# Non-local attention block on one core: reads of the shared PSUM bank moved two steps behind TensorE, a tenth ring slot, four chunks of g ahead of the first image

## The reference

```python
x = x + block(group_norm(x, 32 groups))        # x: 4 images, 256 channels, 4096 positions
# block, for one image, xn = the normalised image as a 256 x 4096 matrix:
g    = g_w @ xn + g_b                          # 128 x 4096
f    = xn.T @ xn                               # 4096 x 4096, symmetric
attn = softmax(f, axis=-1)
y    = attn @ g.T                              # 4096 x 128
wy   = W_w @ y.T + W_b                         # 256 x 4096
wy   = (wy - mean) * rsqrt(var + 1e-5) * gamma + beta   # mean, var over all images and positions
return wy + xn
```

## Time and profile before

| | us |
|---|---|
| median of 3 runs | 2197.24 (2196.96 to 2199.29) |
| profiled execution | 2195.28 |
| its span, first to last instruction | 2193.5 |
| PE busy | 2059.5 (94%) |
| DVE busy | 1556.7 (71%) |
| ACT busy | 1090.8 (50%) |
| POOL busy | 810.7 (37%) |
| chain that ended last | PE 68%, issue 11%, POOL 8%, ACT 5%, DVE 4%, DMA 3% |
| products of f (L1135, L1136, L1137) on PE | 512.8 + 433.1 + 436.1 |
| takes (L930, L938) on DVE | 395.7 + 269.0 |

### The profile page before, as it was taken

The page is one execution under the profiler, slowest core; times in us unless marked ns, Lnnn a source line. Parts: engine busy times, 40 slices in busy tenths (PEclk is TensorE's granted clock), DMA queues, the critical chain, the costliest instruction groups (busy, mean ns, idle before and its releaser), DMA issues.

```text
span 2193.5 us, 32307 instructions
## 1 busy us (share of the span) xinstructions
PE 2059.5 (94%) x9348; PEld 1454.6 (66%) x9348; DVE 1556.7 (71%) x3123; ACT 1090.8 (50%) x2234; POOL 810.7 (37%) x623
## 2 busy tenths in 40 slices
PE   5899999989999999999999999998999999999988
PEld 4686777755577777765667677765558777766433
DVE  5576777777766777786767677777776677777656
ACT  3344455555444445447444445545544444555644
POOL 3001223459602023448631122445850102345840
PEclk9999999999999999999999999999999999999999
DMA  3112234545512323554522223464541233346969
GB/s 139 77 77 81 103 121 130 173 150 178 178 45 87 115 98 110 165 175 138 197 72 93 87 92 112 129 200 137 191 150 49 87 120 102 110 130 218 344 236 356
DMA packets 108408, 304.50 MB, mean 139 GB/s; under 512 B 11584, under 2 KB 11968, under 8 KB 93888
## 3 DMA queue, kind: packets, MB, share of 16 engines
q1 hardware_dynamic: 108224, 302.30, 40.6%
HBM read 159.65 MB, written 142.61 MB: 138 GB/s over the span
## 4 chain that ended last, share of the span: by engine, by line
PE 68%; issue 11%; POOL 8%; ACT 5%; DVE 4%; DMA 3%; DVEq 0%; SPq 0%; POOLq 0%; ACTq 0%
PE bank L1201 12%; PE bank L1135 10%; PE bank L1137 9%; PE bank L1136 9%; PE bank L1177 7%; PE bank L1205 4%; PE bank L1207 4%; PE bank L1206 4%; POOL fy_d L695 3%; POOL fy_c L695 3%; ACT ring L760 2%; PE bank L1350 2%; PE bank L1271 2%; DVE plo L965 2%; DMA fy_c<-spill 2%
## 5 line engine op out<-in xcount | busy, mean ns | idle before, releaser
L786 ACT CAST phi<-bank 128x512 fp32r<-128x512 f32 x480 | 281.9, 588 | 765.7 <-PE bank L1177 764.7
L930 DVE TENSOR_SCALAR_CACHE_REDUCE ring<-bank 128x512 f32<-128x512 f32 x576 | 395.7, 688 | 209.3 <-PE bank L1137 164.0
L1135 PE MATMUL bank<-xh 128*128 128x512 f32 (+3 forms) x1152 | 512.8, 445 | 8.4 <-POOL xl L668 6.4
L1137 PE MATMUL bank<-xh,xl 128*128 128x512 f32 (+3 forms) x1152 | 436.1, 379 | 0.0
L965 DVE TENSOR_TENSOR plo<-bank,phi 128x512 fp32r<-128x512 f32 x480 | 327.2, 685 | 153.5 <-ACT phi L786 121.2
L1136 PE MATMUL bank<-xl,xh 128*128 128x512 f32 (+3 forms) x1152 | 433.1, 376 | 0.0
L1177 PEld LDWEIGHTS bank<-ident,ring 128*128 128x128 f32 x1920 | 231.6, 142 | 183.4 <-issue 109.2
L760 ACT ACTIVATE ring<-ring,nmax 128x512 f32<-128x512 f32 x480 | 345.8, 722 | 0.0
L1177 PE MATMUL bank<-ident,ring 128*128 128x128 f32 x1920 | 295.1, 277 | 43.7 <-DVE plo L965 22.5
L695 POOL TENSOR_TENSOR fy_d<-fy_d,maxrow 128x512 f32<-128x512 f32 x188 | 242.3, 1291 | 222.3 <-DMA fy_d<-spill 222.3
L695 POOL TENSOR_TENSOR fy_c<-fy_c,maxrow 128x512 f32<-128x512 f32 x200 | 259.0, 1297 | 167.0 <-DMA fy_c<-spill 166.6
(11 more groups left out here) (115 smaller groups left out, 2716.9 us busy)
## 6 DMA issues: line engine op xcount, KB each, us to landing
spill<-ring SPq DMA_DIRECT2D x112, 1024.0 KB, 4.4
fy_c<-spill SPq DMA_DIRECT2D x200, 256.0 KB, 4.1
fy_d<-spill SPq DMA_DIRECT2D x188, 256.0 KB, 4.1
ring<-x_dram SPq DMA_DIRECT2D x40, 512.0 KB, 4.9
lbuf<-spill SPq DMA_DIRECT2D x60, 256.0 KB, 4.0
yd<-yn SPq DMA_DIRECT2D x32, 256.0 KB, 3.4
fx_a<-x_dram SPq DMA_DIRECT2D x16, 512.0 KB, 8.3
out_dram<-fx_a SPq DMA_DIRECT2D x16, 512.0 KB, 4.6
```

The lines of the kernel that those rows point to most:

```text
L786: nc.scalar.copy(phi[:, HI_BUF[n], :], whole(p)).then_inc(hi_made, 1)
L930: last = nc.vector.tensor_scalar(ring[:, SLOT[u], t, :], src, 1.0, None, ALU.mult, ALU.max, accum_out=rowm[:, t, c:c + 1])
L1135: nc.tensor.matmul(dst, xh[:, k, rows], xh[:, k, cols], start=(k == 0), stop=False)
L1137: last = nc.tensor.matmul(dst, xl[:, k, rows], xh[:, k, cols], start=False, stop=(k == K - 1))
```

## The change

- `add_g`, `count_wy` and, for rows 1 to 5, `merge_max` move from one step to two steps after PE's part (`merge_max` after the last take: from 0 or 1 to 2). `count_wy` and `invert` move ahead of the takes, `invert` also ahead of the additions of left tiles.
- g: both halves of a chunk are made in one step, the second in the bank `lacc` instead of `sps`. In the head of image 0 four chunks (`FIRST_G`) instead of two are made before the first step, and the exponentials (from step -7) stand ahead of `gh` on ACT.
- A tenth slot, which lies in the first two rows each of `fy_c` and `fy_d`. Only chunk (1, 4) uses it. Products of row 1 are spread over 22 steps instead of 25: the last is made in step 21 (before: 25), of row 2 in step 50 (before: 53).
- The first exponentials of the next image start in step 249 instead of 251, one in each step.
- Normalising starts one step later (`GROUP_AT`), and the cast (`make_xh`) follows the normalisation (`make_xn`) by a step.

```diff
-SLOTS = 9
+SLOTS = 10
+ROW_SLOT = 9
@@ SLOT
-        8, 0, 4, 1, 5, 6, 7,
-        2, 3, 8, 0, 4, 1,
-        5, 6, 7, 2, 3,
+        8, 0, 4, 9, 1, 5, 6,
+        7, 2, 3, 8, 0, 4,
+        5, 6, 7, 1, 2,
@@ plan_products
-        steps = range(PRODUCTS_FROM[j], PRODUCTS_FROM[j] + {1: 25, 2: 19, 3: 18, 4: 18, 5: 18, 6: 2 * n, 7: 2 * n}[j])
+        steps = range(PRODUCTS_FROM[j], PRODUCTS_FROM[j] + {1: 22, 2: 19, 3: 18, 4: 18, 5: 18, 6: 2 * n, 7: 2 * n}[j])
-            step = where[q * len(where) // n]
+            step = where[q * len(where) // n] if j > 1 else steps[q * len(steps) // n]
+            if c == j and t > 1:
+                step = max(step, made[-1] + 1)
+            if SLOT[u] == ROW_SLOT:
+                step = max(step, 2 * T)
-MERGE_STEP = {j: COLS_STEP[j] + (1 if j > 1 else 0) for j in range(1, NB)}
+MERGE_STEP = {j: COLS_STEP[j] + (2 if j < 6 else 1) for j in range(1, NB)}
-FIRST_EXP = -5
+FIRST_EXP = -7
-GROUP_AT = STATS_STEP[-1] + 2
+GROUP_AT = STATS_STEP[-1] + 3
-G_AT = {T * (c - 1) - 2 + h: (c, h) for c in range(2, NB) for h in range(2)}
+G_AT = {T * (c - 1) - (1 if c < NB - 1 else 0): c for c in range(2, NB)}
-SPARE_FROM = {c: max(p for p in SPLIT if tile(p)[1] == c) + 1 for c in range(NB - 1)}
+SPARE_FROM = {c: last_use(LAST_IN_SLOT[ROW_SLOT]) + 1 if c < 2 else max(p for p in SPLIT if tile(p)[1] == c) + 1
+              for c in range(NB - 1)}
-LAST_HEAD_G = G_AT[max(s for s in G_AT if s < HEAD)]
+LAST_HEAD_G = G_AT[max(s for s in G_AT if s < HEAD)], 0
+FIRST_G = range(LAST_HEAD_G[0])
@@ send, on SP
+                if SLOT[u] == ROW_SLOT:
+                    for h, rows in enumerate((fy_c, fy_d)):
+                        sp.dma_start(spill[pair(*CHUNKS[u]), :, 2 * h:2 * h + 2, :],
+                                     rows[:, 0:2 * W].rearrange("p (t w) -> p t w", w=W)).then_inc(spilled[ROW_SLOT], 16)
@@ step, on ACT
-                if s - 1 in G_AT and G_AT[s - 1][1] == 1:
-                    make_gh(b, G_AT[s - 1][0], first)
+                if s - 2 in G_AT:
+                    make_gh(b, G_AT[s - 2], first)
-                    make_xh(b + 1, XN_OF[s])
+                    make_xn(b + 1, XN_OF[s])
+                if more and s - 1 in XN_OF:
+                    make_xh(b + 1, XN_OF[s - 1])
@@ head, on ACT
-            for c in NEXT_G:
-                make_gh(0, c, first=True)
             for s in range(FIRST_EXP, 0):
                 for x3 in EXPS_AT[s]:
                     exp_right(0, *x3)
+                if s + LAG == 0:
+                    for c in NEXT_G:
+                        make_gh(0, c, first=True)
@@ add_g, on DVE (make_g on PE likewise)
+                made = lacc if h == 1 and (first or c not in NEXT_G) else sps
@@ step, on DVE
                 if p in SPLIT_NO:
                     split_lo(b, p, first)
+                if j >= 1 and i == INVERT_AT + LATE[j - 1]:
+                    invert(b, j - 1)
+                if tail and i == INVERT_AT + 1:
+                    invert(b - 1, NB - 1)
                 for w in ADDS_AT[p]:
                     add_left(b, w)
-                if p - 1 in G_AT:
-                    add_g(b, *G_AT[p - 1])
+                if p - 2 in G_AT and not (first and G_AT[p - 2] in FIRST_G):
+                    for h in range(2):
+                        add_g(b, G_AT[p - 2], h)
                 if more and p - 1 in NEXT_G_AT:
                     add_g(b + 1, *NEXT_G_AT[p - 1])
-                if j >= 1 and i == INVERT_AT + LATE[j - 1]:
-                    invert(b, j - 1)
+                if j >= 1 and i - 2 in WY_AT:
+                    count_wy(b, j - 1, WY_AT.index(i - 2))
...
-                if j >= 1 and i - 1 in WY_AT:
-                    count_wy(b, j - 1, WY_AT.index(i - 1))
@@ head, on DVE (on PE likewise)
-            for c in NEXT_G:
+            for c in FIRST_G:
                 for h in range(2):
-                    add_g(0, c, h)
+                    add_g(0, c, h, first=True)
@@ make_g, on PE
+                elif h == 0 or c in NEXT_G:
                     shared_free(b, "g", c, h)
+                elif c > len(NEXT_G):
+                    pe.wait_ge(g_added, b * (2 * NB) + 2 * c)
+                else:
+                    pe.wait_ge(left_taken, b * (NB - 1))
```

66 lines of the change are left out of this document (38 added, 28 removed).

## The result

The changed kernel takes 2146.69 us (median of 4 runs, 2145.51 to 2148.12) against 2197.39 us (4 runs, 2196.96 to 2199.29) of the kernel before: ratio 0.9768, 95% interval 0.9751 to 0.9785. The change wins 50.7 us; 40.7 us were forecast. The time lies in the forecast's own range, 2140 to 2172 us. Not all terms of the sum lie in theirs: blocks 1 to 3 won far more than their upper bound, and block 5 lost time where a gain was forecast.

What follows compares the result with a forecast made beforehand. TensorE, busy 94% of 2193.5 us, bounds the kernel; about 90 us of its waits, apart from the clock, are the ceiling. Terms 12.0+2.8+9.5+3.0+7.8+3.0+5.0-2.4 = 40.7 us, from 2197.24 to 2156.5 us; own range 2140 to 2172, stated range 2140 to 2184.

Steps and rivals of the forecast that it cites:

- End of block 0: Steps 22 to 31, four images: 4.5 us of PE waits less 1.5 for ACT, 3.0 us an image, 12.0 in all.
- the pairs: Pairs of products in steps 8 to 11, two takes a step: cost 0.6 us an image, 2.4 us; bounds 0 and 8.
- Seam: Hardware loop's seam after step 11: a second half of g covers PE's low-half stop; 1.4 us at two seams, 2.8 us.
- Head: Head of image 0: eight halves of g in two banks, exponentials earlier, step 0 at 84.5 us; 9.5 us, bounds 6 and 12.
- The three parts: Head: step 0 earlier 5.0 us, four halves less in later steps 3.7, clock 1.8; together 10.5, less 1.0.
- Blocks 1 to 3: Merges two steps behind shorten PE's waits behind merges and exponentials: 0.75 us an image, 3.0 us; bounds -1 and 6.
- Block 5: Inverse ahead of additions 1.2 us, normalising and cast later 1.4; 2.6 us in three images, 7.8 us; bounds 0 and 14.
- Block 6 and the end of an image: Block 6: 1.0 us in three images, 3.0 us. Image ends: exponentials earlier 2.7, no half clock 2.3, sum 5.0 us.
- (a): DVE's queue bounds more often; only head and image ends gain, 14.5 us, elsewhere waits change name: 2183 us; chance 0.25.
- (b): Slower: PE waits for unread shared bank 7, ten times an image; 55 us loss against 40.7 gain: 2211 us; chance 0.06.
- (c): Block 0: the 22-step product plan does the work, the slot little; changes no time; no chance of its own given.
- One sign that I had named for being wrong: DVE waiting as long as before under another name; no size given.

Runs made afterwards that it cites:

- the two kernels with nine slots: Changed kernel without the tenth slot, with the old product plan: merges near 0.9901, 2175.6 us; merges two steps behind 0.9817, 2157.2 us.
- The square above: Slot against merge distance, near then two steps behind: nine slots 2175.6 and 2157.2 us; ten slots 2170.8 and 2146.4 us (the changed kernel).
- group statistics early: Changed kernel with group statistics and normalising one step earlier, where they were before, the cast still one step behind: 0.9733, 2138.7 us.
- the run with two chunks: Changed kernel with two chunks of g in the head of image 0 instead of four: 0.9771, 2147.1 us.
- merges near: Changed kernel, slot kept, merges where they were before (rows 2 to 5 one step behind the last take, row 1 in its step): 0.9879, 2170.8 us.
- the combined kernel: Changed kernel with group statistics one step earlier, row 6 and 7 merges two steps behind, g chunk 7 in step 22, inverse behind additions: 0.9684, 2128.0 us.
- the kernel with nine slots and far merges: Changed kernel with nine slots and the old product plan, merges still two steps behind the last take: 0.9817, 2157.2 us.
- the kernel with nine slots and near merges: Changed kernel with nine slots, the old product plan and merges where they were before: 0.9901, 2175.6 us.

## Why the prediction was right, and where not

**What bounds the kernel.** Right: the gain came out of PE's waits, for which 90 us were named as the ceiling. Of its clock it kept little: the 20.5 us at half clock in the head, in block 0 and at the end of image 2 are gone, and as many came back around step 176.

**End of block 0.** Forecast 3.0 us an image (4.5 less 1.5 for ACT), and 0.6 us off for the pairs. Blocks 0 of images 1 to 3 won 5.0 to 5.6 us. In steps 26 to 31 one stop of 1.76 us is left of 4.5 us, so that part is 2.8 us, the mechanism and nearly the size. I called ACT late next, with 1.5 us; it is ACT, though by way of GpSimd's low half of g. What I missed lies in front of step 25: steps 0 to 24 fell from 83.70 to 81.80 us, although the transposes of the column maxima moved in, where I had booked a cost of 0.6. The pairs of products cost nothing that shows. The gain in steps 0 to 24 comes neither from the slot nor from the merges: in image 3 steps 0 to 24 take 79.70 and 79.71 us in the two kernels with nine slots, 79.93 in the changed kernel and 82.02 before. Nor from the inverse (79.95 us with it behind again). What is left are g and the projections, to which I had given nothing outside the seam; 0.65 us of it are the projections'. No run takes g's part back by itself. The square above corrects the reason for the rest: I ascribed the gain to the earlier plan; the distance of the merge carries more of it.

**Seam.** Forecast 2.8 us, by an extra 0.92 us of PE to cover the low half. It failed. From step 11 to 13 the seams of images 1 and 2 cost 1.93 and 2.22 us more than the same steps of image 3 before, and 1.89 and 1.93 now: 0.3 us won. After step 11 PE stops 1.68 us (image 1) where it stopped 1.27. First the low half of the kernel before, then the changed kernel:

```profile
644.48 0.69 DVE L965 TENSOR_TENSOR plo<-bank,phi 128x512 fp32r<-128x512 f32 x1 [1.46 <-PE bank L1207]
...
629.60 0.68 DVE L993 TENSOR_TENSOR plo<-bank,phi 128x512 fp32r<-128x512 f32 x1
...
631.41 0.65 PE L1214 MATMUL bank<-ident,ring 128*128 128x128 f32 x4 [1.68 <-issue]
```

The low half ends at 630.28 us, PE starts 1.1 us later with nothing to wait for that the profile shows. In some of the kernels above the profile still names the low half, but there too it ends 0.6 to 1.0 us before PE starts (group statistics early: 625.21 and 626.17 us), while in step 176 of that kernel 0.06 us pass. Already in the kernel before it ended at 645.17 us and PE started at 645.78; the bracket names the releaser, not the distance. So the step that failed is taking this stop for a wait for the low half. It looks like PE's own way through the end of the loop, which covering the low half can't shorten; no run takes the loop away, so this is read from the rows, not tried.

**Head.** Forecast step 0 at 84.5 us; it is at 86.1. But head and block 0 of image 0 won 15.3 us. Less the 5.3 us that other images win in block 0, 10.0 are the head's, against 9.5; by the run with two chunks 2.8 of them hang on the two additional chunks. The three parts shift among themselves: 3.4 us up to step 0 in place of 5.0; the stop in front of it is the 1.05 us below (before: 4.26), and the clock stays at the upper level from 29.6 to 452.9 us, where before it was at half from 83.2 to 93.4 and again from 175.4 to 178.8 us.

```profile
85.71 0.63 PE L1214 MATMUL bank<-ident,ring 128*128 128x128 f32 x4 [1.05 <-DVE plo L993]
```

**Blocks 1 to 3.** Forecast 3.0 us, measured 14.6: the term that was most mis-sized. I took three listed stops and halved them. Two steps' distance is worth 4.6 + 4.8 + 0.8 us there (merges near), reading the projections two steps behind 1.5 us in block 1. The slot with its plan, with far merges, is worth 1.0 us in block 1 and 2.2 in block 2; these parts overlap, so they don't add up exactly to 14.6. I had not seen that the slot ends row 2's products three steps earlier, in step 50; with near merges that brings nothing to block 1 (4.6 us with the slot, 3.8 without), but 2.6 us to block 2.

**Block 4.** Not in the sum. It costs 3.8 us, all by the inverse going ahead, as its undoing shows.

**Block 5.** Forecast a gain of 7.8 us, measured a loss of 3.4. The step that failed is the reading of `GROUP_AT` as a matter of ACT alone. I had moved the normalising, and not counted stage 3 of the statistics on DVE, which moves with it into the step of the merge. ACT's part did come, the stops in steps 189 and 191 (0.41 and 1.24 us) are gone; they are gone in the kernel with the early statistics too, so the shift of `GROUP_AT` bought nothing there. The inverse's 1.2 us did not: its stop is 0.94 us and not gone, and I had left L978 and L998 as long as they were, whatever their order, while the order decides which of the two meets GpSimd.

**Block 6 and the end of an image.** Forecast 1.0 us an image, measured 0.85 in images 0 to 2; but that is some 2.2 us won less the product that came over from block 5, so the agreement is luck. Going ahead brought the inverse 0.41 us of it. Forecast 5.0 us for the ends, measured 7.0: the stop fell from 2.78 to 1.39 us, more than the 0.9 taken, and the half clock after image 2 is gone.

**Rivals.** (a), DVE's queue as the bound, described block 5 rightly and nothing else. (b), PE waiting for unread uses of the shared bank, does not occur: from 28 to 2064 us PE waits for DVE's read of g once, 0.6 us (last line of the waits above). (c) said that the shorter plan does the work in block 0 and the slot little. It stays untested: every run here moves the slot and the plan together. Both together are the smaller part beside the distance of the merges, which (c) did not have. One sign that I had named for being wrong did show in part: DVE waits 111 us less for g and the projections, but 75 us more for the products that it takes (164.0 + 40.7 us before, 222.3 + 57.0 now). That the total came close is partly luck: +11.6 us in blocks 1 to 3 and +9.3 in block 0 and the head met -15.0 us in blocks 4 and 5.

## What to carry to other kernels

A read that two in-order engines share is best placed by the distance at which the data are surely there; for the merges it is that distance, more than an earlier start of the work, that took PE's stops away here. When one constant moves a step, list every engine's instructions that hang on it, and which others share their new step. And put the instruction whose data are ready ahead of the one that has to wait, block by block: the inverse ahead of the additions cost 0.95 us an image in block 4 and won 0.4 in block 6 (1.4 in the combined kernel). And compare blocks only where the clock was the same: a stretch of 3.4 us at half clock hid a gain of 1.9 us in block 0.

## What the hardware showed unexpectedly

An instruction of DVE on 128 x 4 elements took 0.17 us alone and 1.20 us beside a subtraction on GpSimd, without a second input in SBUF, when the subtraction had begun 0.02 to 0.10 us earlier, and 0.17 us when the subtraction began 0.04 us later. Moving an instruction in DVE's queue did not remove such meetings but passed them on: in block 5 the first addition fell from 1.26 to 0.70 us and the sum of the inverse rose from 0.50 to 1.26. In block 4 L1006 takes 1.54 us behind the inverse and 1.62 ahead of it.

PE's clock fell to half at each of the 24 stops of 3.9 us in step 176 over eight kernels, for 6.8 us at 13 of them and for 3.4 us at 11. At shorter stops it was not the same each time: of the three stops of 2.78 us at the end of an image in the kernel before one was followed by half clock, of the three of 2.79 to 2.81 us in the kernel with nine slots and far merges one, of the three of 2.50 us in the kernel with nine slots and near merges two, and of the 26 seam stops of 1.3 to 1.8 us in the 13 kernels with the change of g seven (1.52 to 1.81 us), each for 3.4 us save the first (6.8); the changed kernel, with 1.68 us, kept the upper level. Kernels with the same block 0 differ there by 1.4 to 1.8 us in single images for that reason, so a gain of one or two us is read from the blocks, and not from a median.
